# Relation-aware graph attention: the products of queries and keys in one VectorE operation of 1024 columns instead of two of 512

## The chip, the cores and the metric

The kernel runs on one NeuronCore of one Trainium2 chip. Its time is the device time of one execution in microseconds (us); the median of several runs counts. Before the change it is 1979.32 us (three runs: 1973.38, 1979.32, 1979.64). The profile is one execution, recorded by the hardware. PE is TensorE (matrix products), PEld its loading of weights, DVE is VectorE, ACT is ScalarE, POOL is GpSimd, SP is SyncE, which only issues DMAs here.

## The reference

One layer of attention over a graph with 6250 nodes, 100000 edges, 5 relations, 4 heads of 64 and 256 channels; then a residual and a layer norm without weights.

```python
scale = OUT ** (-0.5)
Q = (jnp.einsum('nc,rch->rnh', x, Wq) + bq[:, None, :]).reshape(R, N, HEADS, OUT)
K = (jnp.einsum('nc,rch->rnh', x, Wk) + bk[:, None, :]).reshape(R, N, HEADS, OUT)
V = (jnp.einsum('nc,rch->rnh', x, Wv) + bv[:, None, :]).reshape(R, N, HEADS, OUT)
q_i = Q[edge_type, dst]
k_j = K[edge_type, src]
v_j = V[edge_type, src]
score = jnp.sum(q_i * k_j, axis=-1) * scale
seg = dst * R + edge_type
m = jax.ops.segment_max(score, seg, num_segments=N * R)
e = jnp.exp(score - m[seg])
s = jax.ops.segment_sum(e, seg, num_segments=N * R)
alpha = e / s[seg]
out = jax.ops.segment_sum(v_j * alpha[..., None], dst, num_segments=N)
x = _layernorm(x + (out.reshape(N, HD) + bias), axis=-1)
```

## The kernel before

The kernel works in three stages. In the first, up to about 770 us, PE makes the tables of queries, keys and values for every node and relation, which go to DRAM, while DVE sorts the edges by target node. The second is the edge stage, which the change touches. The third, from about 1905 us, adds up what crosses chunks, adds x and bias, and normalizes.

The sorted edges lie in 832 tiles of 128, one edge a partition. A step `s` of the edge stage handles four tiles (SB = 4), and there are 208 steps (NSB). Five queues run through the steps, each in its own program order, tied by semaphores:

- POOL gathers the rows of keys and values of four tiles by an indirect DMA each (L504) into a ring of 23 places. It waits for the aggregation of step s - 18 (`s_agg`) and for the products of step s - 5 (`s_mul`).
- SP loads the queries of the four tiles (`qring`, L569) and a row of numbers for the comparison (`bcr`, L562), three steps deep; it waits for the lift of step s - 3 (`s_lift`).
- PE: `lift` (L742) spreads the queries of step s + 1 over the edges by four products with a 0/1 matrix `oht`. They land in `pairs` (called `qk`), two banks of 512 columns. Then `turn_rows` (L689) in some steps, `aggregate` (L730) for the tiles of step q = s - 14, and `turn_carries` (L695, L696). An f32 product shows as two matmul records, so a lift is 8 records and an aggregation 16.
- DVE: `products` (L1245) multiplies keys by lifted queries, reading `pairs`; `scores` (L1251) sums them by head; `payload` (L1312) weights one tile of values; `turned_one_hot` (L1234) and `one_hot` (L1303) make the 0/1 matrices. `add_first` (L1330) adds two columns of a tile's result to `acc` at a place that is in a register: four a step for step q - 2, i = 0 to 3, each of which waits for the one before it (`s_acc`), since two tiles may hit the same column. `weights_a` and `weights_b` are pieces of the softmax over a chunk of eight steps; `weights_a` has a piece in five steps of eight.
- ACT weights the other three tiles of values (L921), moves the aggregated windows to `acc` (L939) and some columns to `cols` (L947), and carries rows and carries of the softmax (L874, L878).

The order on DVE is written out by hand in the loop over s: products of the first half, addition 0, products of the second half, addition 1, the weights' piece, addition 2, scores, payload, the comparison for s + 2, addition 3, `one_hot`, the second weights' piece. `lift(s + 1)` may start when the products of step s have read `pairs`; before the change it does so by halves. The additions begin at step 16 and go on for 16 steps after the last product.

Of the kernel before, what the change touches and what calls it, by code (L numbers as in the profile page):

```python
# [5 lines left out]
P = 128  # L6


def gnn_kernel(nc, x, src, dst, etype, Wq, bq, Wk, bk, Wv, bv, bias, out):
    f32, i32, u16, bf16 = mybir.dt.float32, mybir.dt.int32, mybir.dt.uint16, mybir.dt.bfloat16  # L10
    ALU, ACT, AX = mybir.AluOpType, mybir.ActivationFunctionType, mybir.AxisListType
# [39 lines left out]
    SB = 4  # L51
    NSB = TT // SB
# [6 lines left out]
    KL = 5  # L59
    KS = 23  # L60
    KSTEP = next(k for k in range(1, KS) if k * KL % KS == 1)
    QS = 3
# [83 lines left out]
    with ctx:  # L146
# [87 lines left out]
        ring_k = ring_v[:, C:C + RING].rearrange("p (i l c) -> p i l c", i=SB, l=KS)  # L234
# [19 lines left out]
        qring = cut(QS * SB * C).rearrange("p (s i w) -> p s i w", s=QS, i=SB)  # L254
        bcr = cut(QS * SB * P // 2).bitcast(bf16).rearrange("p (s w) -> p s w", s=QS)
        oht = cut(2 * SB * P).rearrange("p (s w) -> p s w", s=2)
        prod = cut(SB * C).rearrange("p (i w) -> p i w", i=SB)
# [26 lines left out]
        qk = pairs.rearrange("p b (i w) -> p (b i) w", w=C)  # L284
# [26 lines left out]
        s_got = [sem(f"s_got{i}") for i in range(KL)]  # L311
# [47 lines left out]
        def gathered(s):  # L359

            return 16 * SB * (s // KL + 1) - (16 * (TT - USED) if s == NSB - 1 else 0)
# [9 lines left out]
        def spot(s):  # L371

            return KSTEP * s % KS
# [50 lines left out]
        def _(pool):  # L424
# [67 lines left out]
            for s in range(NSB):  # L492
                if s >= KS - KL:

                    pool.wait_ge(s_agg, SB * (s - KS + KL + 1))
                if s >= KL:

                    pool.wait_ge(s_mul, 2 * (s - KL + 1))
                for i in range(SB):
                    t = s * SB + i  # L500
                    if t >= USED:
                        continue
                    a = (i * KS + spot(s)) * C
                    pool.indirect_dma_start(ring_row[:, a:a + 2 * C], None, kv_tab,  # L504
                                            bass.IndirectOffsetOnAxis(ap=kvidx[:, t:t + 1], axis=0)
                                            ).then_inc(s_got[s % KL], 16)
# [9 lines left out]
        @block.sync  # L516
        def _(sp):
            def load_x(t):
                n = nodes(t)
                sp.dma_start(x_sb[0:n, t % XS, :], x[t * P:t * P + n, :]).then_inc(s_x[t % XS], 16)  # L520

            load_x(0)
            sp.wait_ge(s_blank, 3)
            for a, v in ((src_i, src), (typ_i, etype), (dst_i, dst)):
                rows_in = v.rearrange("(p t) -> p t", t=T)
                for lo, hi in ((0, 112), (112, FULL)):
                    sp.dma_start(a[lo:hi, :], rows_in[lo:hi, :]).then_inc(s_edges, 16)
            for t in range(1, XS):
                load_x(t)

            def keep_queries(j):
                sp.wait_ge(s_pq[j % PQ], 16 * (j // PQ + 1))
                sp.dma_start(q_seg_rows[j // RB, j % RB], pq[:, j % PQ, :]).then_inc(s_pqout[j % PQ], 16)

            for t in range(NT):
                if t + XS < NT:
                    sp.wait_ge(s_xT, t + 1)
                    load_x(t + XS)
                if t == 1:
                    for u, b in ((0, bv), (1, bk)):  # L540
                        for q in range(R):
                            sp.dma_start(b_sb[:, (2 * q + u) * C:(2 * q + u + 1) * C],
                                         b[q:q + 1, :].broadcast_to([P, C])).then_inc(s_b, 16)
                wait_added(sp, t)
                for lo, hi in parts(t):
                    sp.dma_start(q_rows[t * P + lo:t * P + hi, :, :],
                                 staged_q(t)[lo:hi, :].rearrange("p (r c) -> p r c", r=R)
                                 ).then_inc(s_qout[t % 3], 16)
            for o in range(NOQ, OA):
                t, r = (o - NOQ) // R, (o - NOQ) % R  # L550
                wait_added(sp, NT + o - NOQ)
                sp.dma_start(kv_rows[t * P:(t + 1) * P, r, :], early[early_slot(o)]
                             ).then_inc(s_early[early_slot(o)], 16)
            for j in range(NQ):
                keep_queries(j)
            sp.wait_ge(s_ready, 1)
            sp.wait_ge(s_base, 16)
            for s in range(NSB):
                if s >= QS:

                    sp.wait_ge(s_lift, 2 * (s - QS + 1))
                sp.dma_start(bcr[:, s % QS, :],  # L562
                             rel_rows[s * SB * P:(s + 1) * SB * P].rearrange("(o w) -> o w", o=1).broadcast_to([P, SB * P])
                             ).then_inc(s_rel[s % QS], 16)
                _, at = nc.values_load_multi_w_load_instructions(
                    base_row[0:1, s * SB:(s + 1) * SB], engines=[SPE], min_val=0, max_val=(NQ - 1) * P,
                    skip_runtime_bounds_check_because="the program limits them")
                for i in range(SB):
                    sp.dma_start(qring[:, s % QS, i, :], q_seg[bass.ds(at[i], P), :]).then_inc(s_gotq[s % QS], 16)  # L569


            sp.wait_ge(s_lift, 2 * NSB)
            sp.dma_start(bias_sb[:], bias.rearrange("(o c) -> o c", o=1).broadcast_to([P, C])).then_inc(s_bias, 16)

            def load_xf(t):
                for lo, hi in parts(t):
                    sp.dma_start(xf[lo:hi, t % XQ, :], x[t * P + lo:t * P + hi, :]).then_inc(s_xf[t % XQ], 16)

            for t in range(XQ):
                load_xf(t)  # L580
            for u in range(NT + 4):
                if u + XQ < NT:
                    sp.wait_ge(s_y, u + 1)
                    load_xf(u + XQ)
                t = u - 4
                if t >= 0:
                    sp.wait_ge(s_o, t + 1)
                    for lo, hi in parts(t):
                        sp.dma_start(out[t * P + lo:t * P + hi, :], of[lo:hi, t % 8, :]).then_inc(s_of[t % 8], 16)
            for i in range(8):  # L590
                sp.wait_ge(s_of[i], 16 * (len(range(i, NT, 8)) + (1 if (NT - 1) % 8 == i else 0)))

        @block.tensor
        def _(pe):
# [139 lines left out]
            def lift(s):  # L734

                pe.wait_ge(s_gotq[s % QS], 16 * SB * (s // QS + 1))
                pe.wait_ge(s_oht, s + 1)
                for half in range(2):
                    if s > 0:
                        pe.wait_ge(s_mul, 2 * (s - 1) + half + 1)  # L740
                    for i in (2 * half, 2 * half + 1):
                        done = nc.tensor.matmul(qk[:, i, :], oht[:, s % 2, i * P:(i + 1) * P], qring[:, s % QS, i, :],  # L742
                                                start=True, stop=True)
                    done.then_inc(s_lift, 1)

            pe.wait_ge(s_ready, 1)
            lift(0)
# [246 lines left out]
        def _(dve):  # L994
# [234 lines left out]
            def turned_one_hot(s):  # L1229

                dve.wait_ge(s_rel[s % QS], 16 * (s // QS + 1))
                if s >= 2:
                    dve.wait_ge(s_lift, 2 * (s - 1))
                nc.vector.tensor_scalar(oht[:, s % 2, :], bcr[:, s % QS, :], part_f[:, 0:1], None, ALU.is_equal  # L1234
                                        ).then_inc(s_oht, 1)

            def products(s, half):

                if half == 0:
                    dve.wait_ge(s_got[s % KL], gathered(s))  # L1240
                dve.wait_ge(s_lift, 2 * s + half + 1)
                if s > 0:
                    dve.wait_ge(s_sc, s)
                two = slice(2 * half, 2 * half + 2)
                nc.vector.tensor_tensor(prod[:, two, :], ring_k[:, two, spot(s), :], qk[:, two, :], ALU.mult  # L1245
                                        ).then_inc(s_mul, 1)

            def scores(s):
                dve.wait_ge(s_mul, 2 * s + 2)
                g = SB * (s % PERC)  # L1250
                nc.vector.tensor_reduce(sc[:, (s // PERC) % 2, :, g:g + SB].rearrange("p h g -> p g h"),  # L1251
                                        prod.rearrange("p i (h d) -> p i h d", h=H), AX.X, ALU.add).then_inc(s_sc, 1)
# [84 lines left out]
            for s in range(NSB + LAG + 2):  # L1337
# [2 lines left out]
                if adds and q % 2 == 0:  # L1340
                    at = load_nodes(q - 2)
                if s < NSB:
                    products(s, 0)
                if adds:
                    dve.wait_ge(s_cols, q - 1)
                    add_first(q - 2, 0, at)
                if s < NSB:
                    products(s, 1)
                if adds:
                    add_first(q - 2, 1, at)  # L1350
                weights_a(s)
                if adds:
# [141 lines left out]
```

## Time and profile before

| | |
|---|---|
| median of three runs | 1979.32 us |
| span of the profiled execution | 1977.2 us |
| DVE busy over the span | 1597.6 us (81%) |
| PE busy over the span | 1614.3 us (82%) |
| POOL busy over the span | 1192.8 us (60%) |
| ACT busy over the span | 1042.2 us (53%) |
| mean granted clock of TensorE | 0.954 of full speed |

The span is that of the profiled execution, from its first to its last instruction; what lies around it is in the median only. The page cuts the span into 40 slices of 49.4 us. Slices 17 to 37 are the edge stage. A group in a view by lines adds up all instructions of one source line, with the mean length of one and with the idle time of the engine just ahead of them. Consecutive operations on DVE overlap in the records: the recorded length of one goes past the start of the next, so what an operation costs is the distance from its start to the next start.

### The profile page before, as it was taken

The numbers are of one execution on the slowest core, as the hardware profiler recorded it, in microseconds if no ns is written. First come the engines' busy times: TensorE is split into PE (matmuls) and PEld (weight loads), VectorE is DVE, ScalarE is ACT, GpSimd is POOL, SyncE is SP. The second block draws the span as 40 slices with busy tenths as digits, with TensorE's granted clock in tenths as the row PEclk, the third lists the DMA queues.
The fourth block names the chain that finished last, engine by engine and source line by source line (L and its number), as shares of the span: only waits on it lengthen the run. The fifth ranks groups of instructions, "written<-read, shape, count | busy, mean of one in ns | idle before, by whom it ended". The sixth has DMA issues, their size and how long they took to land.

```text
span 1977.2 us, 32984 instructions
## 1 busy us (share of the span) xinstructions
PE 1614.3 (82%) x7427; PEld 1118.3 (57%) x7427; DVE 1597.6 (81%) x4148; ACT 1042.2 (53%) x4032; POOL 1192.8 (60%) x1278
## 2 busy tenths in 40 slices
PE   5999889999999994777878877788788877778645
PEld 2455444444444443566667666676666666666634
DVE  7888897544443344799999999999999999999757
ACT  1333322210000000388888888888888888888625
POOL 2111114677777756777777777777777777776105
PEclk9999999999999997799999999999999999999778
DMA  8999999799999999999999999999999999998007
GB/s 223 276 257 265 244 253 247 244 342 364 362 363 363 364 348 312 336 337 328 331 332 318 334 338 327 331 324 333 330 328 326 324 336 338 325 333 287 25 14 226
DMA packets 349631, 592.55 MB, mean 300 GB/s; under 512 B 45391, under 2 KB 240157, under 8 KB 349434
## 3 DMA queue, kind: packets, MB, share of 16 engines
q0 software_dynamic: 90800, 293.85, 47.0%
q1 hardware_dynamic: 224310, 233.25, 35.8%
q10 hardware_dynamic: 34324, 63.35, 8.9%
q8 instruction: 60, 0.98, 0.2%
q14 instruction: 137, 1.12, 0.2%
HBM read 412.09 MB, written 140.94 MB: 280 GB/s over the span
## 4 chain that ended last, share of the span: by engine, by line
PE 29%; DVE 29%; issue 16%; DMA 11%; POOL 9%; DVEq 3%; ACT 2%; SPq 1%; ACTq 0%; POOLq 0%
PE sums L665 21%; POOL region L504 8%; DVE region L1303 6%; DVE region L1245 5%; PE pairs L742 5%; DMA region<-region 4%; DVE region L1037 4%; DVE region L1234 3%; DMA q_tab<-region 3%; DVE acc L1330 3%; PE sums L730 2%; DVEq L1321 2%; DVE region L1312 2%; DMA region<-in_x 1%; DMA region<-kv_tab,kvidx 1%
## 5 line engine op out<-in xcount | busy, mean ns | idle before, releaser
L504 POOL DMA_INDIRECT region<-kv_tab,kvidx x831 | 803.1, 966 | 289.1 <-issue 230.1
L665 PE MATMUL sums<-region,acc 128*128 128x512 f32 (+2 forms) x1568 | 664.9, 577 | 28.4 <-ACT acc L806 21.1
L921 ACT ACTIVATE region<-region 128x64 f32<-128x64 f32 x2392 | 662.5, 346 | 0.8
L742 PE MATMUL pairs<-region 128*128 128x256 f32 x1664 | 437.3, 408 | 197.2 <-DVE region L1245 180.2
L665 PEld LDWEIGHTS sums<-region,acc 128*128 128x128 f32 (+1 forms) x1568 | 292.7, 192 | 335.1 <-issue 289.5
L742 PEld LDWEIGHTS pairs<-region 128*128 128x128 f32 x1664 | 314.7, 199 | 268.8 <-issue 220.4
L730 PE MATMUL sums<-region 128*128 128x131 f32 x3328 | 429.9, 283 | 33.8 <-issue 23.3
L730 PEld LDWEIGHTS sums<-region 128*128 128x128 f32 x3328 | 411.6, 196 | 64.8 <-issue 47.5
L1211 DVE TENSOR_TENSOR region<-sums,region 128x512 f32<-128x512 f32 (+1 forms) x225 | 155.0, 691 | 234.4 <-PE sums L665 230.8
L939 ACT COPY acc<-sums 128x256 f32 x832 | 302.3, 363 | 57.3 <-PE sums L730 53.4
L486 POOL DMA_INDIRECT region<-q_tab,region x288 | 273.1, 948 | 91.0 <-issue 65.9
L1245 DVE TENSOR_TENSOR region<-region,pairs 128x512 f32<-128x512 f32 x416 | 277.4, 672 | 20.6 <-DMA region<-kv_tab,kvidx 19.9
L1251 DVE TENSOR_REDUCE region<-region 128x16 f32<-128x1024 f32 x208 | 252.4, 1214 | 0.9 <-issue 0.2
L898 ACT COPY region<-bank 128x128 f32<-128x128 f32 x26 | 6.9, 265 | 388.7 <-PE bank L709 387.8
L1303 DVE TENSOR_SCALAR region<-iota_f,nrel 128x131 f32<-128x131 f32 x832 | 203.9, 322 | 4.0 <-PE sums L730 3.9
L826 ACT COPY region<-sums 128x512 f32<-128x512 f32 (+1 forms) x167 | 86.3, 527 | 227.5 <-PE sums L665 106.5
L1037 DVE TENSOR_TENSOR region<-region 128x512 f32<-128x512 f32 x292 | 188.9, 688 | 5.1
L454 POOL DMA_DIRECT2D region<-region x49 | 43.2, 883 | 245.9 <-ACT region L826 245.9
L1330 DVE TENSOR_TENSOR acc<-acc,region 128x2 f32 x832 | 128.2, 154 | 20.4 <-ACT region L947 6.7
L1234 DVE TENSOR_SCALAR region<-region,part_f 128x512 f32<-128x512 bf16 x208 | 106.3, 511 | 8.5 <-DMA region<-rel_tab 8.5
L513 POOL TENSOR_TENSOR region<-region 128x256 f32<-128x256 f32 (+1 forms) x49 | 35.4, 731 | 112.4 <-DMA region<-in_x 111.8
L1312 DVE TENSOR_TENSOR region<-region 128x256 f32<-128x256 f32 x234 | 95.7, 418 | 1.1 <-ACT region L912 1.1
(239 smaller groups left out, 901.6 us busy)
## 6 DMA issues: line engine op xcount, KB each, us to landing
region<-q_seg SPq DMA_DIRECT2D x832, 128.0 KB
kv_tab<-region ACTq DMA_DIRECT2D x44, 1280.0 KB, 7.7
q_seg<-region SPq DMA_DIRECT2D x288, 128.0 KB, 5.5
region<-region POOLq DMA_DIRECT2D x48, 640.0 KB, 6.7
q_tab<-region SPq DMA_DIRECT2D x48, 640.0 KB, 5.9
region<-rel_tab SPq DMA_DIRECT2D x208, 128.0 KB
region<-kv_tab,kvidx POOLq DMA_INDIRECT x831
region<-in_x SPq DMA_DIRECT2D x96, 128.0 KB, 3.4
```

What stands on the lines that cost most here:

```text
L486: pool.indirect_dma_start(pq[:, j % PQ, :], None, q_tab, bass.IndirectOffsetOnAxis(ap=seg_list[:, j:j + 1], axis=0)).then_inc(s_pq[j % PQ] ...
L504: pool.indirect_dma_start(ring_row[:, a:a + 2 * C], None, kv_tab, bass.IndirectOffsetOnAxis(ap=kvidx[:, t:t + 1], axis=0)).then_inc(s_got[ ...
L665: done = nc.tensor.matmul(bank[o % 4][0:n, 0:w], acc[:, k, t * P:t * P + n], w_sb[:, k, :, :].rearrange("p u c -> p (u c)")[:, c0:c0 + w], ...
L730: done = nc.tensor.matmul(bank[i][:, h * W:(h + 1) * W], ring_v[:, i, spot(q), h * P:(h + 1) * P], oneh[:, q % 2, i, :], start=True, stop= ...
L742: done = nc.tensor.matmul(qk[:, i, :], oht[:, s % 2, i * P:(i + 1) * P], qring[:, s % QS, i, :], start=True, stop=True)
L921: done = nc.scalar.activation(ring_v[:, i, spot(q), h * D:(h + 1) * D], ring_v[:, i, spot(q), h * D:(h + 1) * D], ACT.Copy, scale=alT[:, h ...
L939: nc.scalar.copy(acc[:, :, bass.ds(at[(q % 2) * SB + i] + 1, P)], bank[i][:, 0:2 * W].rearrange("p (h n) -> p h n", h=2)[:, :, 0:P]).then_ ...
L1037: nc.vector.tensor_tensor(to[:, :, half, :], one, other_half, ALU.max if half else ALU.min).then_inc(s_sort, 1)
L1245: nc.vector.tensor_tensor(prod[:, two, :], ring_k[:, two, spot(s), :], qk[:, two, :], ALU.mult).then_inc(s_mul, 1)
L1251: nc.vector.tensor_reduce(sc[:, (s // PERC) % 2, :, g:g + SB].rearrange("p h g -> p g h"), prod.rearrange("p i (h d) -> p i h d", h=H), AX ...
L1303: done = nc.vector.tensor_scalar(oneh[:, q % 2, i, :], iota_f[:, 1:W + 1], nrel[:, t:t + 1], None, ALU.is_equal)
L1330: nc.vector.tensor_tensor(acc[:, :, bass.ds(col, 1)], acc[:, :, bass.ds(col, 1)], cols[:, q % CS, i, :, 2:3], ALU.add).then_inc(s_acc, 1)
```

## The change

One `tensor_tensor` multiplies all four tiles, 1024 columns across both banks of `pairs`, and signals `s_mul` once. PE's lift waits once, for the whole product of the step before, makes its four products and signals `s_lift` once. All who wait for either semaphore count steps instead of halves. In DVE's loop the second `products` call between additions 0 and 1 is gone, and they follow one another.

```diff
@@ GpSimd
-                    pool.wait_ge(s_mul, 2 * (s - KL + 1))
+                    pool.wait_ge(s_mul, s - KL + 1)
@@ SyncE
-                    sp.wait_ge(s_lift, 2 * (s - QS + 1))
+                    sp.wait_ge(s_lift, s - QS + 1)
@@ TensorE, lift(s)
                 pe.wait_ge(s_oht, s + 1)
-                for half in range(2):
-                    if s > 0:
-                        pe.wait_ge(s_mul, 2 * (s - 1) + half + 1)
-                    for i in (2 * half, 2 * half + 1):
-                        done = nc.tensor.matmul(qk[:, i, :], oht[:, s % 2, i * P:(i + 1) * P], qring[:, s % QS, i, :],
-                                                start=True, stop=True)
-                    done.then_inc(s_lift, 1)
+                if s > 0:
+                    pe.wait_ge(s_mul, s)
+                for i in range(SB):
+                    done = nc.tensor.matmul(qk[:, i, :], oht[:, s % 2, i * P:(i + 1) * P], qring[:, s % QS, i, :],
+                                            start=True, stop=True)
+                done.then_inc(s_lift, 1)
@@ VectorE
-            def products(s, half):
-
-                if half == 0:
-                    dve.wait_ge(s_got[s % KL], gathered(s))
-                dve.wait_ge(s_lift, 2 * s + half + 1)
+            def products(s):
+
+                dve.wait_ge(s_got[s % KL], gathered(s))
+                dve.wait_ge(s_lift, s + 1)
                 if s > 0:
                     dve.wait_ge(s_sc, s)
-                two = slice(2 * half, 2 * half + 2)
-                nc.vector.tensor_tensor(prod[:, two, :], ring_k[:, two, spot(s), :], qk[:, two, :], ALU.mult
-                                        ).then_inc(s_mul, 1)
+                nc.vector.tensor_tensor(prod[:], ring_k[:, :, spot(s), :], qk[:], ALU.mult).then_inc(s_mul, 1)
@@ VectorE, loop over s
                 if s < NSB:
-                    products(s, 0)
+                    products(s)
                 if adds:
                     dve.wait_ge(s_cols, q - 1)
                     add_first(q - 2, 0, at)
-                if s < NSB:
-                    products(s, 1)
-                if adds:
                     add_first(q - 2, 1, at)
                 weights_a(s)
```

The instructions on DVE at step 101, in the middle of the edge stage, a step without a weights piece. ISA is the register instruction that computes the column's address for an addition; what is in brackets are the semaphores it waits for (s_lifted is the lift's). Before:

```order
L1303 TENSOR_SCALAR region<-iota_f,nrel 128x131 [waits s_agg]
L1303 TENSOR_SCALAR region<-iota_f,nrel 128x131 x3
L1245 TENSOR_TENSOR region<-region,pairs 128x512 [waits s_sc,s_lifted,s_got1]
L1330 ISA [waits s_acc,s_cols]
L1330 TENSOR_TENSOR acc<-acc,region 128x2
L1245 TENSOR_TENSOR region<-region,pairs 128x512 [waits s_sc,s_lifted]
L1330 ISA [waits s_acc]
L1330 TENSOR_TENSOR acc<-acc,region 128x2
L1330 ISA [waits s_acc]
L1330 TENSOR_TENSOR acc<-acc,region 128x2
L1251 TENSOR_REDUCE region<-region 128x4x4 [waits s_mul]
```

And the same step on DVE after the change, where lines are numbered three to four lower:

```order
L1299 TENSOR_SCALAR region<-iota_f,nrel 128x131 [waits s_agg]
L1299 TENSOR_SCALAR region<-iota_f,nrel 128x131 x3
L1242 TENSOR_TENSOR region<-region,pairs 128x1024 [waits s_sc,s_lifted,s_got1]
L1326 ISA [waits s_acc,s_cols]
L1326 TENSOR_TENSOR acc<-acc,region 128x2
L1326 ISA [waits s_acc]
L1326 TENSOR_TENSOR acc<-acc,region 128x2
L1326 ISA [waits s_acc]
L1326 TENSOR_TENSOR acc<-acc,region 128x2
L1247 TENSOR_REDUCE region<-region 128x4x4 [waits s_mul]
```

One product is gone, and additions 0, 1 and 2 stand one behind the other, each with its wait for the addition before.

On PE, the lift for step 102 between the turning of the weights and the aggregation, before:

```order
L717 MATMUL bank<-ident,region 128x128 [waits s_al]
L742 MATMUL pairs<-region 128x256 [waits s_mul,s_oht,s_gotq0]
L742 MATMUL pairs<-region 128x256
L742 MATMUL pairs<-region 128x256 [waits s_mul]
L742 MATMUL pairs<-region 128x256
L730 MATMUL sums<-region 128x131 [waits s_pay,s_cols,s_oh]
```

And after:

```order
L717 MATMUL bank<-ident,region 128x128 [waits s_al]
L741 MATMUL pairs<-region 128x256 [waits s_mul,s_oht,s_gotq0]
L741 MATMUL pairs<-region 128x256 x3
L730 MATMUL sums<-region 128x131 [waits s_pay,s_cols,s_oh]
```

The order of the matmuls is the same; the second wait for the products is gone, and the first one is for the whole step.

## Rows read from the trace of the kernel before

**Rows 1.** The page: busy us and share by engine, and DVE's busy tenths by slice.
```profile
PE 1614.3 (82%) x7427; PEld 1118.3 (57%) x7427; DVE 1597.6 (81%) x4148; ACT 1042.2 (53%) x4032; POOL 1192.8 (60%) x1278
...
DVE  7888897544443344799999999999999999999757
```

**Rows 2.** Busy time by window: start:end, length, then by engine; clock, DMA.
```profile
core 0: us, PE busy (x) PEld busy (x) DVE busy (x) ACT busy (x) POOL busy (x), PEclk, DMA share, GB/s
770.00:845.00 75.00, 50.60 (x187) 37.72 (x187) 54.73 (x110) 19.62 (x78) 56.73 (x60) 0.75 1.00 344
...
1000.00:1800.00 800.00, 631.94 (x3968) 547.00 (x3968) 787.06 (x2389) 675.63 (x2790) 594.78 (x616) 0.98 0.98 330
```

**Rows 3.** Waits: total us, times, longest; first row 770:1000, the rest 1000:1800.
```profile
DVE region L1245 <- DMA region<-kv_tab,kvidx: 16.0, 8, 2.8
...
DVE region L1261 <- ACT region L874: 0.7, 1, 0.7
DVE region L1251 <- issue: 0.2, 1, 0.2
...
POOL region L504 <- issue: 169.2, 553, 0.5
POOL region L504 <- PE sums L730: 32.1, 49, 2.6
POOL region L504 <- DVE region L1245: 4.3, 14, 0.3
```

**Rows 4.** Groups by line, 1000:1800: count, busy us, mean ns, idle before.
```profile
L504 POOL DMA_INDIRECT region<-kv_tab,kvidx x616 | 595.5, 967 | 205.5 <-issue 169.2 <-PE sums L730 32.1 <-DVE region L1245 4.3
...
L1251 DVE TENSOR_REDUCE region<-region 128x16 f32<-128x1024 f32 x154 | 186.9, 1214 | 0.5 <-issue 0.2
...
L1330 DVE TENSOR_TENSOR acc<-acc,region 128x2 f32 x616 | 93.7, 152 | 7.6
```

**Rows 5.** Timeline of step 101: start us, us, engine, line.
```profile
1281.60 0.68 DVE L1245 TENSOR_TENSOR region<-region,pairs 128x512 f32<-128x512 f32 x1
...
1282.20 0.15 DVE L1330 TENSOR_TENSOR acc<-acc,region 128x2 f32 x1
1282.27 0.68 DVE L1245 TENSOR_TENSOR region<-region,pairs 128x512 f32<-128x512 f32 x1
...
1282.43 1.97 PE L742 MATMUL pairs<-region 128*128 128x256 f32 x8 [1.50 <-DVE region L1245]
...
1282.87 0.45 DVE L1330 TENSOR_TENSOR acc<-acc,region 128x2 f32 x2
1283.23 1.21 DVE L1251 TENSOR_REDUCE region<-region 128x16 f32<-128x1024 f32 x1
...
1284.36 0.41 DVE L1312 TENSOR_TENSOR region<-region 128x256 f32<-128x256 f32 x1
...
1284.69 0.48 DVE L1234 TENSOR_SCALAR region<-region,part_f 128x512 f32<-128x512 bf16 x1
...
1285.95 0.68 DVE L1245 TENSOR_TENSOR region<-region,pairs 128x512 f32<-128x512 f32 x1
```

**Rows 6.** Line L1330, 1281.5:1287.5: duration min/median/max in ns.
```profile
L1330 DVE TENSOR_TENSOR acc<-acc,region x6: 151/154/163, 1282.2 to 1287.2; 128x2 f32 x6
L1330 DVEq FUSED_REGOPS  x6: 46/46/46, 1282.4 to 1287.4; - x6
```

**Rows 7.** Timeline from 1308.4, a step with a weights piece.
```profile
1308.20 1.03 PE L742 MATMUL pairs<-region 128*128 128x256 f32 x4
...
1309.70 0.57 ACT L874 COPY region<-bank 1x512 f32<-1x512 f32 x1 [1.63 <-PE bank L689]
...
1311.27 0.41 DVE L1261 TENSOR_TENSOR_SCAN region<-region 1x128 f32<-1x128 f32 x1
```

**Rows 8.** Critical chain within 1300:1320, shares by line.
```profile
by line: PE pairs L742 28.1%; issue 17.9%; DVE region L1303 14.2%; DVE region L1245 11.6%; DVE region L1234 7.5%; DVEq L1321 6.0%; DVE region L1312 3.4%; DVE region L1262 3.1%; DVE acc L1330 2.7%; DVE region L1261 2.5%; DVE region L1251 2.1
```

More of the change, by code:

```diff
@@ L569, in _ @@
                     sp.dma_start(qring[:, s % QS, i, :], q_seg[bass.ds(at[i], P), :]).then_inc(s_gotq[s % QS], 16)
-            sp.wait_ge(s_lift, 2 * NSB)
+            sp.wait_ge(s_lift, NSB)
             sp.dma_start(bias_sb[:], bias.rearrange("(o c) -> o c", o=1).broadcast_to([P, C])).then_inc(s_bias, 16)
@@ L1232, in turned_one_hot @@
                 if s >= 2:
-                    dve.wait_ge(s_lift, 2 * (s - 1))
+                    dve.wait_ge(s_lift, s - 1)
                 nc.vector.tensor_scalar(oht[:, s % 2, :], bcr[:, s % QS, :], part_f[:, 0:1], None, ALU.is_equal
                                         ).then_inc(s_oht, 1)
-            def products(s, half):
-                if half == 0:
-                    dve.wait_ge(s_got[s % KL], gathered(s))
-                dve.wait_ge(s_lift, 2 * s + half + 1)
+            def products(s):
+                dve.wait_ge(s_got[s % KL], gathered(s))
+                dve.wait_ge(s_lift, s + 1)
                 if s > 0:
                     dve.wait_ge(s_sc, s)
-                two = slice(2 * half, 2 * half + 2)
-                nc.vector.tensor_tensor(prod[:, two, :], ring_k[:, two, spot(s), :], qk[:, two, :], ALU.mult
-                                        ).then_inc(s_mul, 1)
+                nc.vector.tensor_tensor(prod[:], ring_k[:, :, spot(s), :], qk[:], ALU.mult).then_inc(s_mul, 1)
             def scores(s):
-                dve.wait_ge(s_mul, 2 * s + 2)
+                dve.wait_ge(s_mul, s + 1)
                 g = SB * (s % PERC)
```

## The prediction

> **What bounds the kernel now.** I read the page's shares and slices first, then a table of windows, then the waits and the groups of the long middle stretch, and last the timeline of single steps. The page shows no engine full over the whole run: PE 82%, DVE 81% [rows 1]. The slices show why that average misleads: after the sort and the projections, DVE stands at nine tenths without a break, from slice 18 on to slice 37. The windows give it in numbers [rows 2]: from 1000 to 1800 us DVE is busy 787.06 of 800 us (98.4%), PE 631.94, ACT 675.63, POOL 594.78. L1251 runs 154 times there [rows 4], once a step, so a step takes 800 / 154 = 5.19 us, and 208 of them make the edge stage.
>
> Busy alone does not make DVE the bound, since the DMA share is 0.98 as well and POOL issues gathers all the time. So the waits decide [rows 3]. In 800 us DVE waited for others 0.7 + 0.2 us, and not once for gathered rows. POOL, on the other hand, waited 32.1 us for PE and 4.3 us for DVE before it could issue gathers: it is held back by its consumers. Its own work is 595.5 us of issues [rows 4] and 169.2 us of gaps between them [rows 3], 765 of 800 us or 4.97 us a step. DVE sets the pace, and the gathers have some 4% in hand. Between 770 and 1000 us DVE did wait for gathers, 16.0 us in 8 times [rows 3]; there the ring fills.
>
> **The change part by part.** In one step DVE runs, in this order, two products, four additions to acc (L1330) spread between the others, the sum of the products (L1251), payload, two kinds of comparison, and in five steps of eight a piece of the weights. The change touches three things there.
>
> *One product instead of two.* In the timeline of one step [rows 5] the first product starts at 1281.60 and the addition behind it at 1282.20; the second starts at 1282.27, its addition at 1282.87, 0.60 us later both times. The recorded 0.68 us of each overlap the next instruction. What one operation of 1024 columns takes stands in the same rows: L1251 starts at 1283.23 and its successor at 1284.36, 1.13 us. It reads 1024 columns of f32 too, though from the region alone. A second way: L1312 with 256 columns has its successor 0.33 us behind (1284.36 to 1284.69), a product with 512 has it 0.60 behind, so 256 columns cost 0.27 us and 1024 come to 0.60 + 2 x 0.27 = 1.14. The trace has no operation of 1024 columns that reads pairs, so I bound it on both sides: below by 1.07, twice what 512 columns cost without what an operation adds (2 x 0.54), above by 1.20 (both halves added, no gain at all). I take 1.13, the row of the same width. Saved: 0.60 + 0.60 - 1.13 = 0.07 us a step.
>
> *The additions lose what lay between them.* Each addition carries a wait for the one before it (s_acc) on a register instruction that computes its address, and that instruction is the sequencer's. The product that stood between additions 0 and 1 hid this wait. The trace has additions with nothing between them, in the steps without a weights piece: the row at 1282.87 is two of them, 0.45 us in all [rows 5]. A single one takes 0.151 to 0.163 us [rows 6]; with 0.163 for the second, it started 0.287 us after the first. An addition followed by anything else costs 0.07 us until the next start (1282.20 to 1282.27). So an addition directly behind another costs 0.287 - 0.07 = 0.217 us more. The group of 1000 to 1800 us says the same from another side. Three steps of eight have no weights piece, 58 of 154, and in each DVE idles 0.287 - 0.154 = 0.13 us ahead of the second addition, 7.5 us together; the group has 7.6 us of idle time ahead of L1330 [rows 4]. After the change addition 1 stands directly behind addition 0 in every step that has products and additions, so 0.217 us are added a step, and where there is no weights piece three stand in a row. Bounds: at least 0, if the wait were free here; at most 0.287, a whole start-to-start.
>
> The Trainium skill speaks against this term: "VectorE: DVE Perf Modes", The DRAIN you can't avoid, says that a semaphore between chained operations costs nothing extra, and its rules for kernel authors say to minimize the count of operations, not of semaphores. By that rule the change would be a plain gain of 0.07 us a step, and the sum about -14 us instead of +28. The trace, with 0.45 us for the two additions, disagrees: here the wait is on an instruction of the sequencer ahead of the addition.
>
> *The signal once a step.* PE's first two matmuls of the next lift waited for the first product only, and now wait for both. The lift begins 0.15 us after the first product's recorded end: at 1282.43 after 1282.28 [rows 5]. The first product ended 0.68 us after its start, the merged one ends about 1.21 us after it, so the lift starts and ends 0.53 us later against the product. Who waits for it? The next product, first of all. In that step the lift ends at 1282.43 + 1.97 = 1284.40 and the next product starts at 1285.95, 1.55 us later. After the change that margin is 1.55 - 0.53 + 0.15 = 1.17 us. Behind the waiting lift PE has in its queue the turning of the rows, the aggregation and the turned carries. PE is busy 632 of 800 us [rows 2], 4.1 us a step, so it has 1.1 us idle to take the 0.53 from, and a step gets 0.15 longer. The carry chain is the tightest [rows 7]: the lift ends at 1309.23, L874 on ACT ends at 1309.70 + 0.57 = 1310.27, and DVE uses it at 1311.27: 1.00 us in hand, and 1.00 - 0.53 + 0.15 = 0.6 after. Aggregation starts up to 0.53 us later, and POOL waits for it (the 32.1 us); but POOL has a later step's demand to meet too, and its 4% grow with a slower DVE. SP's loads of q_seg wait for the lift and have two steps' time. I put this part at 0, with 0.53 us a step as the bound where no margin held; one wait of 0.7 us for ACT in 800 us [rows 3] says that such margins are seldom used up.
>
> **The sum.** Per step +0.217 - 0.07 = +0.147 us. It applies where a step has products and additions: additions begin at step 16, products end with step 207, 192 steps, 192 x 0.147 = 28.2 us. In steps 0 to 15 only the 0.07 us are saved, 1 us together, where DVE partly waits for gathers anyway; I count 0.5. The 16 steps behind the last product have their additions back to back in both kernels. Together +27.7 us. The profiled execution has a span of 1977.2 us; the median of the runs is 1979.3, so about 2.1 us lie around it. 1977.2 + 2.1 + 27.7 = 2007 us, 1.4% slower.
>
> **The rivals.**
>
> *The wait is free and the merge pays (faster).* If DVE hid the wait between additions, only the product's saving is left: 208 x 0.07 = 14.6 us, 1965 us. For it: DVE is the bound, so every saved start-up counts in full. Against it: the 0.45 us row and the 7.6 us of idle time. It decides from a penalty under 0.07 us, a third of what the rows show.
>
> *The gathers are the bound (no change).* If POOL and the DMA queues set the 5.19 us, DVE's 0.15 us vanish in time that it would wait. For it: the DMA share of 0.98 [rows 2], and that a step like the one shown takes DVE 4.35 us (1281.60 to 1285.95), less than the gathers' 4.97, so that only the lead of the ring feeds three such steps in a row. Against it: DVE has no wait for a gather in 1000 to 1800 us [rows 3]. 1979 us, within 0.3%.
>
> *The late lift takes over (much slower).* PE's chain from product to lift to the next product gets longer by 0.53 us. For it: the critical chain of 1300 to 1320 us lies 28.1% on L742 [rows 8], and the granted clock dips at times (0.98 mean in the middle window, 0.75 between 770 and 845 us [rows 2]); where it is at the lower of its two levels, 1.2 instead of 2.4 GHz, the lift's matmuls stretch. Against it: at full clock 1.17 us are left. If it decided in a quarter of the steps, 48 x 0.53 = 25 us would come on top: 2032 us. It decides from a lift that takes over 3.1 us instead of 2.
>
> **How the numbers follow.** A difference under 0.3%, 6 us, can't be told from none here: the three runs of before spread over 6.3 us. My forecast gets 0.82, with its own range 2001 to 2013: the product's upper bound would add 0.07 x 192 = 13 us, its lower one take off 0.06 x 192 = 12, the additions' upper bound 0.07 x 192 = 13 us, and of each I let in half. The free wait gets 0.06, the bound gathers 0.06, the late lift 0.06. Faster by over 0.3% then 0.06, within 0.3% 0.06, slower 0.88. The range reaches up some way to the late lift and to the two upper bounds, and down to half of the additions' penalty hidden (0.108 x 192 = 21 us less would be 1986, of which it takes in half): 1996 to 2018.
>
> **What would show it.** In the profile after: 208 products of 128x1024, mean near 1.21 us recorded, successors 1.13 us behind; in the timeline of a step without weights three additions in one row of some 0.73 us (0.45 + 0.287); idle time ahead of the additions in 1000 to 1800 us up from 7.6 us by 0.13 x 150, to about 27; steps of 5.35 us on average; PE's and POOL's waits longer, and DVE still with no wait for gathers. Wrong it would be if DVE showed new waits for PE at the product (the late lift), if additions in a row took under 0.2 us each, or if the step stayed at 5.19 us with DVE waiting for gathers.

## The result and the profile after

The changed kernel takes 2019.72 us (median of four runs, 2015.56 to 2021.20), the kernel before 1977.87 us in the same comparison: a ratio of 1.0214, 95% interval 1.0199 to 1.0228. It is slower, as forecast, but by 42 us where 28 were forecast, and its time lies outside the range of 1996 to 2018 us.

The window of 1000 to 1800 us of the kernel after, with the columns of [rows 2]:

```profile
core 0: us, PE busy (x) PEld busy (x) DVE busy (x) ACT busy (x) POOL busy (x), PEclk, DMA share, GB/s
...
1000.00:1800.00 800.00, 624.46 (x3815) 539.33 (x3814) 759.76 (x2143) 644.54 (x2684) 571.79 (x592) 0.96 0.95 316
```

DVE is busy 759.76 us where it was 787.06, so it has gaps now. The groups by line of that window show one kind of gap (columns as in [rows 4]):

```profile
L504 POOL DMA_INDIRECT region<-kv_tab,kvidx x592 | 573.5, 969 | 228.5 <-issue 161.4 <-PE sums L730 61.0 <-DVE region L1242 6.2
...
L1247 DVE TENSOR_REDUCE region<-region 128x16 f32<-128x1024 f32 x148 | 179.7, 1214 | 0.0
L1242 DVE TENSOR_TENSOR region<-region,pairs 128x1024 f32<-128x1024 f32 x148 | 178.2, 1204 | 0.0
...
L1326 DVE TENSOR_TENSOR acc<-acc,region 128x2 f32 x591 | 94.2, 159 | 27.1 <-DVE acc L1326 0.5
```

There are 148 steps in 800 us where there were 154, 5.41 us each. The product takes 1.204 us (1.21 forecast). The idle time ahead of the additions went from 7.6 us [rows 4] to 27.1 (27 forecast). The timeline of a step without a weights piece, DVE alone, answers to [rows 5]:

```profile
1301.57 1.22 DVE L1242 TENSOR_TENSOR region<-region,pairs 128x1024 f32<-128x1024 f32 x1
1302.70 0.76 DVE L1326 TENSOR_TENSOR acc<-acc,region 128x2 f32 x3
1303.37 1.22 DVE L1247 TENSOR_REDUCE region<-region 128x16 f32<-128x1024 f32 x1
1304.50 0.42 DVE L1308 TENSOR_TENSOR region<-region 128x256 f32<-128x256 f32 x1
```

The product's successor starts 1.13 us behind it, and three additions in a row take 0.76 us (0.73 forecast). The second kind of gap stands in the waits of DVE and POOL, 1000 to 1800 us, columns as in [rows 3]:

```profile
POOL region L504 <- issue: 161.4, 527, 0.5
...
POOL region L504 <- PE sums L730: 61.0, 59, 2.9
...
DVE region L1257 <- ACT region L873: 9.0, 12, 0.9
```

L1257 (L1261 before) is the carry scan of the softmax, once in each of the first and third steps of a chunk of eight. It waited once for 0.7 us before, now 12 times, 9.0 us together. That is the chain which the prediction called the tightest and then left at nothing. The timeline of one third step shows why (PE, DVE and ACT):

```profile
1673.63 1.20 DVE L1242 TENSOR_TENSOR region<-region,pairs 128x1024 f32<-128x1024 f32 x1
...
1674.97 3.35 PE L741 MATMUL pairs<-region 128*128 128x256 f32 x8 [2.13 <-DVE region L1242]
...
1678.12 0.63 PE L689 MATMUL bank<-ident,region 128*1 128x128 f32 x2
...
1679.10 0.57 ACT L873 COPY region<-bank 1x512 f32<-1x512 f32 x1 [3.87 <-PE bank L689]
...
1679.70 0.41 DVE L1257 TENSOR_TENSOR_SCAN region<-region 1x128 f32<-1x128 f32 x1 [0.91 <-ACT region L873]
```

The lift takes 3.35 us and not 1.97. ACT has the row at 1679.67, and DVE, which stood ready at 1678.79, scans 0.91 us late. In another chunk the same step runs as forecast:

```profile
1632.34 1.97 PE L741 MATMUL pairs<-region 128*128 128x256 f32 x8 [2.14 <-DVE region L1242]
...
1634.79 0.57 ACT L873 COPY region<-bank 1x512 f32<-1x512 f32 x1 [2.20 <-PE bank L689]
...
1635.97 0.41 DVE L1257 TENSOR_TENSOR_SCAN region<-region 1x128 f32<-1x128 f32 x1
```

Here ACT has the row at 1634.79 + 0.57 = 1635.36, and 1635.97 - 1635.36 = 0.61 us are in hand, the forecast's 0.6. What differs is TensorE's clock. Windows over both lifts, with the columns of [rows 2] (behind the length and the five busy times comes the granted clock):

```profile
1632.00:1634.00 2.00, 1.66 (x8) 1.50 (x9) 1.87 (x7) 0.59 (x4) 1.39 (x3) 1.00 1.00 339
1674.90:1676.90 2.00, 1.93 (x6) 1.56 (x7) 1.87 (x6) 0.32 (x2) 1.46 (x2) 0.62 0.89 319
1676.90:1679.00 2.10, 2.10 (x9) 1.35 (x8) 1.89 (x8) 0.00 (x0) 1.49 (x3) 0.55 1.04 374
```

In the slow lift the clock is mostly at its lower level of 1.2 GHz (half of 2.4). PE had stood idle for 2.13 us ahead of it, but for 2.14 us ahead of the fast one too, so the idle time just ahead of a lift does not decide by itself; what decides between two chunks is open. The Trainium skill, "TensorE: Matmul & The Clock Gate", What's actually happening, says that the throttled state is the default and that activity releases it; the runs agree in direction, with 15 of 22 third lifts slow here and none in e3, where PE has extra work in this gap.

The third step can be followed in the 22 chunks between 850 and 1810 us, by the records of its lift and by the distance from its sum of products (L1247, L1251 before) to that of the next step. "Stage" is the time from the first to the last of the 208 sums of products. Each row is one execution.

| run | PE idle ahead of the third step's lift, median us | its lifts over 2.3 us | the step's length, mean us | stage, us |
|---|---|---|---|---|
| before | 1.78 | 2 of 22 | 6.35 | 1072.9 |
| after | 2.13 | 15 of 22 | 7.12 | 1115.2 |
| e1_late_lift | 2.01 | 8 of 22 | 6.72 | 1089.1 |
| e2_adjacent | 1.91 | 11 of 22 | 6.61 | 1114.9 |
| e3_filled | 1.24 | 0 of 22 | 6.44 | 1097.9 |
| e6_late_filled | 1.12 | 0 of 22 | 6.27 | 1076.0 |
| e7_before_filled | 0.88 | 0 of 22 | 6.26 | 1073.6 |

The kernel before has slow lifts too, 9 of 22 in the fifth step. There nothing on DVE waits behind the lift, and they cost nothing. Of the two slow third lifts of the kernel before, one is the wait of 0.7 us in [rows 3], which the prediction took as a sign that such margins are seldom used up:

```profile
1432.04 3.39 PE L742 MATMUL pairs<-region 128*128 128x256 f32 x8 [1.91 <-DVE region L1245]
...
1436.77 0.41 DVE L1261 TENSOR_TENSOR_SCAN region<-region 1x128 f32<-1x128 f32 x1 [0.72 <-ACT region L874]
```

```profile
1432.00:1434.00 2.00, 1.96 (x6) 1.61 (x7) 2.00 (x6) 0.72 (x4) 1.70 (x2) 0.60 1.01 363
```

The granted clock was 0.60 there. So the kernel before had this wait already, in 2 of 22 chunks.

### The profile page after: what moved, and what is told of

Read it like the earlier page. It is cut to its first block, busy times and chain, and to the rows that moved or that the text cites. A ratio compares the mean times of both kernels' runs of the same rounds, so it can differ in the third digit from the quotient of the medians.

```text
span 2019.1 us, 32569 instructions
## 1 busy us (share of the span) xinstructions
PE 1631.6 (81%) x7427; PEld 1131.9 (56%) x7427; DVE 1602.8 (79%) x3940; ACT 1035.5 (51%) x4032; POOL 1194.1 (59%) x1278
## 4 chain that ended last, share of the span: by engine, by line
PE 38%; DVE 35%; DMA 10%; issue 10%; DVEq 3%; POOL 3%; ACT 2%; SPq 1%; ACTq 0%; POOLq 0%
PE sums L665 20%; PE pairs L741 11%; DVE region L1242 10%; DVE region L1299 6%; DMA region<-region 4%; PE sums L730 4%; DVE region L1036 4%; DVE region L1233 3%; DMA q_tab<-region 3%; DVE acc L1326 2%; POOL region L504 2%; DVE region L1252 2%; DVEq L1317 2%; DMA region<-in_x 1%; DVE region L1308 1%
## 5 line engine op out<-in xcount | busy, mean ns | idle before, releaser
L741 PE MATMUL pairs<-region 128*128 128x256 f32 x1664 | 455.2, 420 | 243.0 <-DVE region L1242 226.2
L741 PEld LDWEIGHTS pairs<-region 128*128 128x128 f32 x1664 | 324.0, 205 | 321.0 <-issue 267.2
L730 PE MATMUL sums<-region 128*128 128x131 f32 x3328 | 425.2, 281 | 30.4 <-issue 19.6
L1242 DVE TENSOR_TENSOR region<-region,pairs 128x1024 f32<-128x1024 f32 x208 | 250.7, 1205 | 21.1 <-PE pairs L741 12.5
L1247 DVE TENSOR_REDUCE region<-region 128x16 f32<-128x1024 f32 x208 | 252.5, 1214 | 0.5
L1299 DVE TENSOR_SCALAR region<-iota_f,nrel 128x131 f32<-128x131 f32 x832 | 194.6, 308 | 3.7 <-PE sums L730 3.7
L1326 DVE TENSOR_TENSOR acc<-acc,region 128x2 f32 x832 | 133.6, 161 | 46.1 <-ACT region L946 6.8
```

The costliest lines, as they stand in the source:

```text
L730: done = nc.tensor.matmul(bank[i][:, h * W:(h + 1) * W], ring_v[:, i, spot(q), h * P:(h + 1) * P], oneh[:, q % 2, i, :], start=True, stop= ...
L1242: nc.vector.tensor_tensor(prod[:], ring_k[:, :, spot(s), :], qk[:], ALU.mult).then_inc(s_mul, 1)
L1299: done = nc.vector.tensor_scalar(oneh[:, q % 2, i, :], iota_f[:, 1:W + 1], nrel[:, t:t + 1], None, ALU.is_equal)
L1326: nc.vector.tensor_tensor(acc[:, :, bass.ds(col, 1)], acc[:, :, bass.ds(col, 1)], cols[:, q % CS, i, :, 2:3], ALU.add).then_inc(s_acc, 1)
```

## The experiments

Theory A: the additions cost what the prediction says, and the missing 14 us are TensorE's lower clock in the third step, which makes the carry scan late. Theory B: they are the late lift as such.

**e1_late_lift** keeps the change's signals and undoes the merge and the adjacency. In DVE's loop (the halves also get a semaphore of their own for the scores):

```diff
-                    products(s)
+                    products(s, 0)
                 if adds:
                     dve.wait_ge(s_cols, q - 1)
                     add_first(q - 2, 0, at)
+                if s < NSB:
+                    products(s, 1)
+                if adds:
                     add_first(q - 2, 1, at)
```

> The change's signals without its merged product: DVE multiplies by halves again with addition 0 between them, but PE's lift waits for both halves and signals once a step. Theory A (back-to-back additions cost 28 us, and a longer step leaves PE idle longer, which drops TensorE's clock at the lift of a chunk's third step and costs 14 more): DVE's step is as before, the lift starts 0.53 us later, PE's idle time ahead of it stays as before (1.8 us), the lift of the third step stays at 1.97 us; 1978 us, within 4 of the kernel before. Theory B (the 14 us beyond the forecast come from the late lift itself): about 1992 us, with DVE waiting at the carry scan in most chunks.

Measured: 1994.31 us, ratio 1.0070 (1.0049 to 1.0092), 14 us slower by the ratio. Theory A as I put it fell: with DVE's work as before, the late lift alone makes PE's idle time longer (2.01 us) and 8 of 22 third lifts slow. Theory B's number came out, and its mechanism only by half, as e6 shows.

**e2_adjacent** does the opposite, early lifts and the additions adjacent:

```diff
                     products(s, 0)
+                    products(s, 1)
                 if adds:
                     dve.wait_ge(s_cols, q - 1)
                     add_first(q - 2, 0, at)
-                if s < NSB:
-                    products(s, 1)
-                if adds:
                     add_first(q - 2, 1, at)
```

> The kernel before with both halves of the product first and additions 0 and 1 behind them, halves signalled apart as before. Theory A: 192 steps x 0.217 us for the additions = 42 us, so 2020 us; the step is longer than in the change, so PE idles longer and its clock drops at the third step at least as often; as the lift starts at 0.82 us and not at 1.35, DVE's carry scan has 0.5 us more and waits only 0.4 us a time, up to 7 us on top: 2020 to 2027 us. Theory B: 2020 us, no slow lifts at the third step. A free wait between additions: 1978 us.

Measured: 2016.83 us, ratio 1.0185 (1.0165 to 1.0206), 37 us slower, 33 to 41 by the interval, where 42 to 49 were expected. The number is a little short of Theory A's, but the wait between additions is the main cost. It is not free, against the first rival. The Trainium skill ("VectorE: DVE Perf Modes", The DRAIN you can't avoid) says of a chain of copies that the semaphore between them costs nothing extra; for these small additions, whose wait is on a register instruction, this run shows otherwise. The longer step drops the clock too, 11 of 22, but the lift starts early enough for the scan to wait only 2.3 us in 6 times, between 845 and 1800 us:

```profile
DVE region L1261 <- ACT region L874: 2.3, 6, 0.5
```

**e3_filled** adds work for PE in the gap of the changed kernel; bank 6's columns from 256 on are used by nothing else:

```diff
                 if k == 1:
                     turn_carries(c, 0)
+                if k == 2:
+                    for _ in range(4):
+                        nc.tensor.matmul(bank[6][:, 2 * P:3 * P], ident[:], ident[:], start=True, stop=True)
                 if k == 3:
```

> The changed kernel with four more matmuls of the unit matrix by itself (about 1 us, output never read) on PE behind the aggregation of each chunk's second step, where PE is idle for 2.1 us ahead of the lift. Theory A: lifts of the third step are back at 1.97 us, DVE's wait at the carry scan goes, about 0.63 us x 26 chunks = 16 us less: 2004 us. Theory B: the clock is no part of it, 2020 us as the change.

Measured: 2006.63 us, ratio 1.0139 (1.0116 to 1.0162). Against the change's 1.0214 that is 15 us less, for 1 us more of work a chunk. The timeline of a third step has the extra matmuls (L715), the full-speed lift and the scan without a wait:

```profile
1659.58 1.05 PE L715 MATMUL bank<-ident 128*128 128x128 f32 x8
...
1661.88 1.97 PE L744 MATMUL pairs<-region 128*128 128x256 f32 x8 [1.25 <-DVE region L1245]
...
1664.33 0.57 ACT L876 COPY region<-bank 1x512 f32<-1x512 f32 x1 [2.20 <-PE bank L689]
1665.62 0.40 DVE L1260 TENSOR_TENSOR_SCAN region<-region 1x128 f32<-1x128 f32 x1
```

What is left, 27 us, agrees with the prediction's sum of 27.7 (23 to 32 by the interval).

**e4_merged_spread** puts something between any two additions of the changed kernel. The order of DVE in a step becomes:

```diff
                     add_first(q - 2, 0, at)
-                    add_first(q - 2, 1, at)
                 weights_a(s)
+                if s + 2 < NSB:
+                    turned_one_hot(s + 2)
                 if adds:
-                    add_first(q - 2, 2, at)
+                    add_first(q - 2, 1, at)
                 if s < NSB:
                     scores(s)
+                if adds:
+                    add_first(q - 2, 2, at)
                 if 0 <= u < NSB:
                     payload(u)
-                if s + 2 < NSB:
-                    turned_one_hot(s + 2)
```

> The changed kernel with something between any two additions: product, addition 0, weights piece, comparison for s + 2, addition 1, scores, addition 2, payload, addition 3, one_hot. Theory A: no addition behind another, so against the kernel before 0.07 us x 208 for the product and 0.217 us x 72 (192 x 3/8) for the pairs that it already had are saved: 1978 - 15 - 16 = 1947 us; up to 14 more if the clock drops at the third step, though PE idles less in shorter steps. A free wait between additions: 1963 us. Gathers as the bound (4.97 us a step): 1978 - 0.22 x 192 = at least 1936 us.

Measured: 1972.86 us, ratio 0.9975 (0.9959 to 0.9992). Of the expected 31 us only 5 came. The fifth and sixth steps got shorter, 4.13 and 4.18 us for 4.37 and 4.44, but the group of the gathers and DVE's waits, 1000 to 1800 us, show who took it back:

```profile
L504 POOL DMA_INDIRECT region<-kv_tab,kvidx x619 | 612.5, 990 | 188.7 <-issue 155.7 <-PE sums L730 25.0 <-DVE region L1242 7.9
```

```profile
DVE region L1242 <- DMA region<-kv_tab,kvidx: 15.8, 25, 1.4
```

POOL is full: 612.5 + 188.7 = 801 us, and its 188.7 us of idle time are 0.305 us ahead of each of 619 issues, the gap that it has when it waits for nothing; no gap is longer than 0.35 us. One gather costs 1.295 us, a step 5.18.

**e5_halves_spread** is the same on the kernel before, with early lifts:

```diff
                 weights_a(s)
+                if s + 2 < NSB:
+                    turned_one_hot(s + 2)
                 if adds:
                     add_first(q - 2, 2, at)
                 if s < NSB:
                     scores(s)
                 if 0 <= u < NSB:
                     payload(u)
-                if s + 2 < NSB:
-                    turned_one_hot(s + 2)
```

> The kernel before with the comparison for s + 2 moved between additions 1 and 2, so that no addition stands behind another; products, lifts and signals by halves as before. If DVE alone were the bound: 0.217 us x 72 = 16 us less, 1962 us. Theory C, from the run with the merged product spread out: POOL issues its gathers without a pause there, 1.295 us each, 5.18 us a step, so no order on DVE gets the stage below 5.17 us a step against 5.18 before: 1972 to 1976 us, with waits of DVE for gathered rows.

Measured: 1974.83 us, ratio 0.9980 (0.9968 to 0.9992), as theory C has it. DVE waits for gathers in the same window:

```profile
DVE region L1245 <- DMA region<-kv_tab,kvidx: 13.8, 21, 2.1
```

**e6_late_filled** and **e7_before_filled** put e3's matmuls into e1 and into the kernel before; **e8_spread_filled** into e4. Their edit is that of e3.

> Products by halves, lift and signal once a step, and the four extra matmuls of the unit matrix behind the second step's aggregation (output never read). The same without the extra matmuls took 1994 us. If a half of its 16 us is the lower clock at the third step's lift (8 of 22 slow there): the wait at the carry scan goes and 8 us with it, 1986 us; what stays is the wait for the turned scores at a chunk's start, 0.2 us x 26 = 5 us, from the late lift. If the clock has no part in it: 1994 us.

Measured: 1982.98 us, ratio 1.0020 (1.0006 to 1.0035), 4 us slower than before. The clock was 10 of e1's 14 us. The other 4 are the late lift itself: in the first step of a chunk DVE makes the mask PEN (L1273) and then scans the scores that PE has turned, and the scan starts 0.40 us behind PEN on average, 0.44 in e1, 0.25 before: 0.15 x 26 chunks = 4 us. In the changed kernel this cost does not arise: the scan starts 0.24 us behind PEN, since PEN itself starts 1.50 us behind the product's start there and 1.33 in e1.

> The kernel before with the same four extra matmuls. Control: its lifts of the third step run at full clock already (2 of 22 slow) and its slow ones, at the fifth step, have nothing waiting for them. The matmuls should change nothing: 1977 us, within 4.

Measured: 1979.60 us, ratio 1.0001 (0.9989 to 1.0014). The extra matmuls gain nothing by themselves.

> The changed kernel with the additions spread out and the extra matmuls as well. Without the matmuls 1973 us with 3 of 22 slow lifts at the third step. Theory C (gathers at 5.17 us a step): 1971 to 1973 us. If the clock still cost something there, up to 5 us less: 1968 us.

Measured: 1972.94 us, ratio 0.9971 (0.9958 to 0.9983). Like e4 within the intervals; there the gathers set the time, not the clock.

**e9_spread_narrow** and **e10_before_narrow** halve what a gather brings:

```diff
-                    pool.indirect_dma_start(ring_row[:, a:a + 2 * C], None, kv_tab,
+                    pool.indirect_dma_start(ring_row[:, a + C:a + 2 * C], None, kv_half,
```

with `kv_half` the same table seen as rows of 256 columns. The indices stay those of whole rows, so what lands is a half row from another place in the first half of the table, and not the edge's keys as the expectation says; the values are left out. The results are wrong for that reason; the number of gathers and all other work stay the same.

> The merged product with additions spread out, and gathers that bring the 256 columns of keys alone, so half of their bytes; values are left out, what is weighted and aggregated is whatever lies in the ring. If the bytes of the gathers set 5.17 us a step: DVE's savings show in full, 1978 - 15 - 16 + 5 (wait for the turned scores) = 1952 us. If POOL's issues set it whatever they bring (0.967 + 0.305 us each at the least, 5.09 us a step): not under 1963 us. If neither is the bound: 1973 us as with whole rows.

Measured: 1974.06 us, ratio 0.9987 (0.9972 to 1.0002). Window and gathers, 1000 to 1800 us:

```profile
1000.00:1800.00 800.00, 626.16 (x3988) 548.25 (x3986) 777.29 (x2247) 669.41 (x2805) 611.53 (x619) 0.99 0.77 230
```

```profile
L505 POOL DMA_INDIRECT region<-kv_tab,kvidx x619 | 612.0, 989 | 188.7 <-issue 169.5 <-PE sums L731 13.4 <-DVE region L1243 5.8
```

230 GB/s instead of 330, a DMA share of 0.77 instead of 0.98, and the same 619 gathers at 989 ns. The bytes are no bound. That the issues on POOL are, the time alone doesn't tell, since two of the three expectations allow 1974 us; it is the 188.7 us, again 0.305 us ahead of each issue and no gap longer than 0.35.

> The kernel before with the same halved gathers (values left out). DVE is its bound and has no wait for gathers, so halving them should change little: 1978 us, down to 1972 where gathers were late at the start of the stage.

Measured: 1978.11 us, ratio 1.0003 (0.9989 to 1.0017). DVE sets the kernel before, and halved gathers are worth nothing to it.

## Why the prediction was wrong

**What bounds the kernel.** DVE, rightly: halved gathers change nothing in the kernel before (e10), and what e2 adds to DVE comes through, 37 us of 42. "The gathers have some 4% in hand" was too much. The 32.1 us that POOL waited for PE [rows 3] were 49 waits, and each of them contains the 0.3 us that lie between any two issues. With this gap for all of them POOL needs 595.5 + 616 x 0.305 = 783 of 800 us, 5.09 us a step: 2% in hand. Even these went when the additions were spread, since an issue then took 990 ns and not 967, 5.18 us a step. Where the difference lies can be counted in the traces, 1000 to 1800 us: issues whose record overlaps one of DVE's comparisons (L1234, L1303) take 1.018 us on average in e5 (372 of them) and the others 0.948 (245); before, 0.980 (262) and 0.957 (353). So the spread order puts more issues beside a comparison, and they are the long ones; that the comparisons cause it was not tested by a run. The misread margin did not touch the forecast, since the change slowed DVE. The first rival's 1965 us, 5.12 us a step, would have come within 0.03 us of this second bound.

**One product instead of two.** Right: 1.13 us to its successor.

**The additions.** Right: 0.76 us for three, and 27 us of idle time. In the traces of the change and of e3 an addition with another right behind it costs 0.28 to 0.30 us until the next start in seven of the eight steps of a chunk (0.35 in the second), and 0.07 to 0.08 with nearly anything else behind it. With the product, the forecast's sum of 27.7 us is what e3 measured (1.0139, 23 to 32 us by its interval).

**The signal once a step.** This is the step that failed: "I put this part at 0"; it cost some 15 us. Its working held at full clock: the lift starts 1.34 us after the product (1673.63 to 1674.97), and the carry chain keeps 0.61 us. But it took the lift's 1.97 us as fixed. PE's idle time ahead of the third lift grew from 1.78 to 2.13 us, partly by the late lift (2.01 alone, e1), partly by the longer step (1.91 alone, e2); the clock fell in 15 of 22 chunks, the lift came out up to 1.7 us longer, and 0.6 us in hand were too few. The third step is 0.77 us longer than before where 0.147 were forecast: 0.62 x 26 chunks = 16 us, and e3 gives 15 back.

**The rivals.** The third, the late lift with a lower clock, had the right cause, but not its place and price. It looked for the wait at the next product with 1.17 us in hand, so it needed a lift of over 3.1 us and got 0.06. The smaller margin stood in the paragraph on the signal: with 0.6 us in hand at the carry scan, a lift of 2.6 us decides. The second rival (gathers) was wrong for this change and is what stops any gain from spreading the additions.

## What to carry to other kernels

Before two operations on a saturated engine are merged, look at what stood between them: here the second product hid the latency of a chain of dependent additions, and a merge worth 0.07 us uncovered 0.22. A margin measured at full TensorE clock may be none where PE idles just ahead of it: look for the tightest chain behind the lift and price it with the lower clock. Where two engines run within two per cent of each other, read a wait's total without the gap that is there anyway, or the second bound stays hidden until the first is gone.

## What was not expected of the hardware

In the changed kernel PE was busy for 624.46 of 800 us and stood idle for 2.13 us (median) ahead of a third lift, and 15 of 22 of these lifts came out slow, with the granted clock at 0.62 and 0.55 over the one shown; with four small matmuls of 1.05 us together in that gap none did (e3). The clock fell in the kernel before as well, mostly in a step where it cost nothing. A gather issued on POOL costs the same with half of its bytes (989 and 990 ns), while the DMA share falls from 0.98 to 0.77, so a DMA share near one did not mean that the DMA engines were the bound.
